# Three long VectorE products of a graph-attention kernel, each made in four operations

## The chip, the cores and the metric

The kernel runs on one core of a Trainium2 chip. A core has a matrix engine (TensorE, "PE" in the profile, with its weight loads as "PEld"), a vector engine (VectorE, "DVE"), an activation engine (ScalarE, "ACT"), a general engine (GpSimd, "POOL") and a synchronising engine that here only issues DMAs (SyncE, "SP"). The metric is the device time in microseconds of one whole launch: 3388.77 us for the kernel before, the median of three runs (3386.15 to 3389.04).

## What is computed

A graph of N = 3125 nodes with 128 features and E = 50000 edges, sorted by destination, goes through a block of two graph convolutions and then through five graph-attention layers with two heads. A layer of the second kind is, in the reference:

```python
edge_emb = edge_attr_full @ ew.T + eb                 # 16 attributes per edge
xw = x @ W
xj = xw[src].reshape(-1, H, D) + edge_emb.reshape(-1, H, D)
xi = xw[dst].reshape(-1, H, D)
alpha = einsum('ehd,hd->eh', xi, att_i) + einsum('ehd,hd->eh', xj, att_j)
alpha = leaky_relu(alpha, 0.2)
ea = exp(alpha - segment_max(alpha, dst)[dst])
alpha = ea / (segment_sum(ea, dst)[dst] + 1e-16)
aggr = segment_sum(xj * alpha[..., None], dst)
x_next = aggr.mean(axis=1) + b                        # relu between layers
```

So a layer needs, for each edge, the row of its source node (a gather), two attention numbers, an exponential relative to the largest of its destination, and a weighted sum over the edges of each destination.

## The kernel before

Edges stand in tiles of 128, one per partition; 391 tiles hold real edges. Four tiles make a group, and a chunk is 28 tiles, that is seven groups: `CH = [28] * 13 + [16, 11]`, so 15 chunks in a layer and 75 in the five layers. The destinations of one tile fall into a window of WIN = 24 nodes. `onehot` (128 x 392 x 24) says which node of its tile's window an edge goes to.

**GpSimd** fetches the rows. For each tile of a layer, in order, it issues an indirect DMA (line 510) that reads 128 rows of 130 numbers of `table` in HBM into one slot of `ring`, which has 60 slots. Before tile t with t >= 60 it waits at the first tile of each group until TensorE has summed the group that used the slot 60 tiles earlier (`sums`, line 508). Between the layers it adds two halves of S (line 517) and clears tiles of `acc` (line 495).

**ScalarE** copies, per tile, the window of destination terms out of `ai_rows` into `ai_win` (line 580; 28 copies per chunk), and makes the exponentials of a chunk (line 586).

**VectorE** makes the weights. All its work on a chunk is written out in one order:

- `windows_sum(layer, c, part)` in three parts. Part 0 multiplies the chunk's edge attributes `at` (k tiles x 16) by the two heads' vectors into `prod`, 2 x 28 x 16 = 896 numbers per partition (line 1087). Part 1 waits for ScalarE's windows and multiplies `ai_win` by `onehot`, 28 x 2 x 24 = 1344 numbers (line 1091). Part 2 reduces both, over the 16 attributes (line 1093) and over the 24 nodes (line 1094), tells ScalarE that `ai_win` is free (`win_used`), and adds the two (line 1096).
- `chain_scan` waits until all gathers of the chunk have landed (line 1101) and adds the rows' terms (line 1105 or 1108); then come maxima per destination by scans within and across partitions (`chain_scan`, `chain_rows`, `chain_cols`, lines 1111 to 1156).
- `chain_probs` waits for the exponentials, copies them into `est`, and makes the edge terms: attributes times weight, 28 x 2 x 16 = 896 numbers (line 1175). `weigh` then makes the weighted one-hots `pw` of a group (192 numbers, line 1161), which TensorE waits for.
- `add_group` waits for a group's sum in PSUM and adds it into `acc` (line 1200).

The work of chunk c+1 is laid between the groups of chunk c (lines 1228 to 1253): parts 0, 1 and 2 of `windows_sum` stand ahead of the adds of groups 0, 1 and 2, the scan after group 2, rows and columns after group 3, the probabilities after group 5. `weigh` runs four groups ahead of the adds, and six PSUM banks hold sums. For the two short chunks all three parts stand after group 0.

**TensorE** takes the groups in order (`aggregate`, lines 728 to 749): it waits for `weigh`'s semaphore, clears the bank (line 741), and does two products for each tile (lines 745 and 747); after some groups it makes a tile of the self terms (line 783). `link(ins)` on VectorE gives an instruction an increment of the semaphore `step` and makes the engine wait for it; `mark(ins)` gives the increment alone.

Of the kernel before, what the change touches and what calls it, by code (L numbers as in the profile page):

```python
# [5 lines left out]
ALU = mybir.AluOpType  # L6
# [4 lines left out]
AX = mybir.AxisListType.X  # L11

P = 128
# [3 lines left out]
H = 2  # L17
LAYERS = 5
FA = 16
# [6 lines left out]
WIN = 24  # L26
ROW = D + H
REG = 3
HF = H * FA
QD = 32  # L30
EC = HF + 2 * H
BIG = 1e30
# [14 lines left out]
TC = [sum(CH[:c]) for c in range(NC + 1)]  # L47
# [7 lines left out]
NAT = 3  # L55
# [42 lines left out]
def program(nc, x, src_rows, src_key, src_flat, dst_col, dst_next_col, dst_flat, dst_first,  # L98
            attr, W1, b1, W2, b2,
            weights, weightsT, attT, edge_w, edge_b, edge_woT, biases, edge_bias, out):  # L100
    with ExitStack() as ctx:
# [17 lines left out]
        onehot = sb("onehot", [P, TILES, WIN])  # L119
        S = sb("S", [P, NT, H * D])  # L120
        est = sb("est", [P, 2, K, EC])
        at = sb("at", [P, NAT, K, FA])
        ai_win = sb("ai_win", [P, K, H, WIN])
        prod = sb("prod", [P, H * K * FA])
# [7 lines left out]
        alpha = sb("alpha", [P, H, QB])  # L132
# [24 lines left out]
        v17 = sb("v17", [P, LAYERS, H, FA + 1])  # L157
# [15 lines left out]
        ee = bwd[:, :, :].rearrange("p h e -> p (h e)")[:, 0:H * K]  # L173
# [103 lines left out]
        step = sem("step")  # L277
# [58 lines left out]
        est_ready = sem("est_ready")  # L336
        acc_zero = sem("acc_zero")
        win_ready = sem("win_ready")
        win_used = sem("win_used")
# [469 lines left out]
        def _(v):  # L809
            steps = [0]  # L810

            def mark(ins):
                steps[0] += 1
                ins.then_inc(step, 1)
                return steps[0]

            def link(ins):
                v.wait_ge(step, mark(ins))
# [5 lines left out]
            V = nc.vector  # L824
# [7 lines left out]
            link(V.tensor_scalar(phi_mask[:, 0:1], iota_p, float(FA), None, ALU.is_lt))  # L832
            link(V.tensor_scalar(phi_mask[:, 1:2], iota_p, float(HF), None, ALU.is_lt))
            link(V.tensor_tensor(phi_mask[:, 1:2], phi_mask[:, 1:2], phi_mask[:, 0:1], ALU.subtract))
# [112 lines left out]
            for c in range(NPC):  # L947
                pick(c, n_e)
                b, ne = c % 2, n_e[:, c * PC:(c + 1) * PC]
# [71 lines left out]
            for g in range(GCN_G):  # L1021
# [3 lines left out]
                c, i = divmod(g, K // GRP)  # L1025
# [13 lines left out]
                win = acc[:, 0, bass.ds(base[0], GW)]  # L1039
# [40 lines left out]

            def windows_sum(layer, c, part):
                gc, k, hk = layer * NC + c, CH[c], H * CH[c]
                ts = slice(TC[c], TC[c + 1])
                win, pr = ai_win[:, 0:k, :, :], prod[:, 0:hk * FA].rearrange("p (h k f) -> p h k f", h=H, f=FA)
                if part == 0:
                    v.wait_ge(at_in[gc % NAT], 16 * (gc // NAT + 1))
                    link(V.tensor_tensor(pr, at[:, gc % NAT, 0:k, :].unsqueeze(1).broadcast_to((P, H, k, FA)),
                                         v17[:, layer, :, 0:FA].unsqueeze(2).broadcast_to((P, H, k, FA)), ALU.mult))
                if part == 1:
                    v.wait_ge(win_ready, gc + 1)  # L1090
                    link(V.tensor_tensor(win, win, onehot[:, ts, :].unsqueeze(2).broadcast_to((P, k, H, WIN)), ALU.mult))  # L1091
                if part == 2:
                    V.tensor_reduce(ee[:, 0:hk], prod[:, 0:hk * FA].rearrange("p (q f) -> p q f", f=FA), AX, ALU.add)
                    link(V.tensor_reduce(alpha[:, :, 0:k].rearrange("p h k -> p k h"), win, AX, ALU.add))  # L1094
                    v.sem_inc(win_used, 1)
                    link(V.tensor_tensor(alpha[:, :, 0:k], alpha[:, :, 0:k],
                                         ee[:, 0:hk].rearrange("p (h k) -> p h k", h=H), ALU.add))

# [67 lines left out]
            def chain_probs(layer, c):  # L1166
                gc, k, hk = layer * NC + c, CH[c], H * CH[c]
                es = est[:, c % 2, 0:k, :]
                v.wait_ge(exp_al, gc + 1)
                link(V.transpose(probs[:, :, :], dd[:, 0:H * QB].rearrange("p (h e) -> p h e", h=H)))  # L1170
                pr = probs[:, :, 0:k].rearrange("p h k -> p k h")
                done = mark(V.tensor_copy(es[:, :, HF:HF + H], pr))
                V.tensor_tensor(es[:, :, HF + H:EC], maxes[:, :, 0:k].rearrange("p h k -> p k h"),
                                last_col[:, TC[c]:TC[c + 1]].unsqueeze(2).broadcast_to((P, k, H)), ALU.mult)
                V.tensor_tensor(es[:, :, 0:HF].rearrange("p k (h f) -> p k h f", h=H),
                                at[:, gc % NAT, 0:k, :].unsqueeze(2).broadcast_to((P, k, H, FA)),
                                pr.unsqueeze(3).broadcast_to((P, k, H, FA)), ALU.mult).then_inc(est_ready, 1)
                v.wait_ge(step, done)
                for g in GC[c][0:2 if c else AHEAD]:
                    weigh(layer, g)  # L1180
# [22 lines left out]
            for layer in range(LAYERS):  # L1203
# [64 lines left out]
                for q in range(P // QD):  # L1268
                    ins = V.transpose(nsT[q * QD:(q + 1) * QD, :, :],
                                      acc[QD:2 * QD, 2, 0:NP].rearrange("p (j q n) -> p q j n", q=P // QD, n=QD)[:, q, :, :])  # L1270
# [22 lines left out]
                for j in range(NT):  # L1293
# [7 lines left out]
                    if not final and j >= 1:  # L1301
# [3 lines left out]
                    ins = V.scalar_tensor_tensor(out=yj, in0=yb[:, D:2 * D], scalar=c1[:, 1, j:j + 1],  # L1305
                                                 in1=yj, op0=ALU.mult, op1=ALU.add).then_inc(y_sb, 1)
# [71 lines left out]
```

## Time and profile before

| | |
|---|---|
| time, median of 3 runs | 3388.77 us (3386.15 to 3389.04) |
| span of the profiled execution | 3764.7 us, 48376 instructions |
| PE busy | 2439.0 us (65%) |
| POOL busy | 2210.5 us (59%) |
| DVE busy | 2004.0 us (53%) |
| ACT busy | 696.7 us (19%) |
| mean granted TensorE clock of the span | 0.537 |

The span is from the first to the last instruction of one execution recorded by the hardware profiler; the page gives no other time for that execution. It is 376 us longer than the median of the runs without the profiler, so the span and the metric are not the same thing. "Busy" leaves out waiting, semaphore and register instructions. A row of a group gives line, engine, operation, what it writes and reads, how often, then the time in which the group was busy and the mean of one, and the idle time ahead of it with what ended it. "Remote" is an end of waiting that the view can put down to no instruction of the core.

### The profile page before, as it was taken

To read this page: it belongs to the slowest core of one execution; us is meant where nothing else is said; L and a number is where in the kernel's file an instruction comes from. 1 tells how busy PE (TensorE), PEld (TensorE's weight loads), DVE (VectorE), ACT (ScalarE), POOL (GpSimd) and SP (SyncE) were. 2 spreads that over 40 slices of the span, in tenths; PEclk is the share of its full clock that TensorE was granted. 3 is DMA by queue.
4 is the path that set the end of the run, shared out by engine and by line. 5 is a ranking of instruction groups with operands and counts; after the bars stand their busy time and mean duration, and the time that the engine had idled before them with its cause. 6 is when DMAs were issued, how large, how long until landed. Compare 5 with 4: busy or idle time off the path is not lost.

```text
span 3764.7 us, 48376 instructions
## 1 busy us (share of the span) xinstructions
PE 2439.0 (65%) x13595; PEld 2001.4 (53%) x13595; DVE 2004.0 (53%) x6216; ACT 696.7 (19%) x3102; POOL 2210.5 (59%) x2357
## 2 busy tenths in 40 slices
PE   6779726666582766658276665837576582766668
PEld 6679615555461655547165554725455461655546
DVE  8955624554472555547255554725454472555456
ACT  0078511111121111112111111211111121111112
POOL 0067466666626766662666666266676626666661
PEclk8555555555565555556555555655555565555556
DMA  3212122222202222221222222022222202222221
GB/s 101 97 60 80 30 52 54 53 52 57 49 24 51 54 51 53 56 49 30 47 54 52 53 56 49 25 53 54 50 53 57 50 24 50 54 50 53 52 49 40
DMA packets 114121, 195.78 MB, mean 52 GB/s; under 512 B 39897, under 2 KB 77272, under 8 KB 113864
## 3 DMA queue, kind: packets, MB, share of 16 engines
q0 software_dynamic: 62560, 130.25, 15.2%
q1 hardware_dynamic: 51304, 62.42, 5.3%
q8 instruction: 122, 2.00, 0.2%
q14 instruction: 135, 1.11, 0.1%
HBM read 180.86 MB, written 11.67 MB: 51 GB/s over the span
## 4 chain that ended last, share of the span: by engine, by line
DVE 36%; PE 25%; another core or an unknown queue 20%; issue 13%; DVEq 3%; POOL 1%; ACT 1%; ACTq 1%; DMA 0%; POOLq 0%
PE bank L745 10%; PE bank L747 6%; DVE acc L1200 4%; DVE into L1143 2%; DVEq L1016 2%; PE bank L718 2%; DVE pw L1161 2%; DVE alpha L1094 2%; PE bank L741 2%; PE bank L783 2%; DVE fwd L1150 2%; DVE lanes L1129 2%; DVE prod L1072 1%; PE bank L766 1%
## 5 line engine op out<-in xcount | busy, mean ns | idle before, releaser
L510 POOL DMA_INDIRECT ring<-table,srci x1955 | 1941.2, 993 | 937.6 <-issue 556.4
L745 PE MATMUL bank<-pw,ring 128*128 128x48 f32 x3910 | 1210.9, 404 | 203.3 <-issue 201.8
L745 PEld LDWEIGHTS bank<-pw,ring 128*128 128x128 f32 x3910 | 1014.9, 314 | 302.9 <-issue 231.1
L1200 DVE TENSOR_TENSOR acc<-acc,bank 128x288 f32 x490 | 222.8, 455 | 1128.7 <-remote 857.3
L747 PE MATMUL bank<-onehot,est 128*36 128x24 f32 x3910 | 632.6, 243 | 222.9 <-issue 221.7
L741 PE MATMUL bank<-zeros 128*128 128x288 bf16 x490 | 208.5, 426 | 697.1 <-DVE pw L1161 438.7
L747 PEld LDWEIGHTS bank<-onehot,est 128*36 128x36 f32 x3910 | 391.2, 149 | 393.9 <-issue 226.6
L741 PEld LDWEIGHTS bank<-zeros 128*128 128x128 bf16 x490 | 55.4, 113 | 752.0 <-DVE pw L1161 453.3
L586 ACT ACTIVATE dd<-dd 128x66 f32<-128x66 f32 x75 | 19.4, 258 | 2163.4 <-DVE dd L1154 1177.9
L580 ACT COPY ai_win<-ai_rows 128x48 f32 x1955 | 336.3, 229 | 432.6 <-issue 410.5
L491 POOL TENSOR_TENSOR ring<-ring,acc 128x512 f32<-128x512 f32 x98 | 117.1, 1195 | 250.1 <-ACT ring L545 246.7
L517 POOL TENSOR_TENSOR S<-S 128x128 f32<-128x128 f32 x125 | 57.4, 459 | 323.6 <-ACT S L590 319.2
L783 PE MATMUL bank<-Wl,S 128*128 128x258 f32 x250 | 152.8, 697 | 50.1 <-issue 48.7
L718 PE MATMUL bank<-onehot,ring 128*128 128x24 f32 x784 | 172.2, 388 | 18.4 <-ACT ring L556 7.9
L718 PEld LDWEIGHTS bank<-onehot,ring 128*128 128x128 f32 x784 | 169.3, 331 | 21.1 <-DVE bank L1043 8.8
L1091 DVE TENSOR_TENSOR ai_win<-ai_win,onehot 128x1344 f32<-128x1344 f32 (+2 forms) x75 | 109.1, 1455 | 122.5 <-issue 101.2
L1161 DVE TENSOR_TENSOR pw<-onehot,est 128x192 f32<-128x192 f32 x490 | 160.0, 352 | 0.1
L556 ACT ACTIVATE ring<-ring,acc 128x128 f32<-128x128 f32 x392 | 124.3, 389 | 29.4 <-PE bank L718 24.7
L1143 DVE COPY into<-carry 2x96 f32<-2x96 f32 x300 | 93.6, 312 | 45.9 <-issue 33.8
L800 PE MATMUL bank<-El,acc 128*128 128x256 f32 x250 | 95.8, 470 | 23.8 <-DVE y L1305 20.0
L1094 DVE TENSOR_REDUCE alpha<-ai_win 128x56 f32<-128x1344 f32 (+2 forms) x75 | 108.6, 1448 | 0.0
L783 PEld LDWEIGHTS bank<-Wl,S 128*128 128x128 f32 x250 | 64.6, 308 | 70.3 <-issue 63.8
(214 smaller groups left out, 2610.1 us busy)
## 6 DMA issues: line engine op xcount, KB each, us to landing
ring<-table,srci POOLq DMA_INDIRECT x1955
ai_rows<-lo_dram SPq DMA_DIRECT2D x28, 896.0 KB, 4.3
at<-in_attr SPq DMA_DIRECT2D x65, 224.0 KB
table<-ring SPq DMA_DIRECT2D x15, 390.0 KB, 3.5
table<-ring SPq DMA_DIRECT2D x5, 325.0 KB, 3.4
result<-ring SPq DMA_DIRECT2D x24, 64.0 KB
x_mid<-ring SPq DMA_DIRECT2D x3, 384.0 KB, 2.7
table<-ring SPq DMA_DIRECT2D x5, 130.0 KB, 2.4
```

The source lines that it names most:

```text
L510: nc.gpsimd.indirect_dma_start(out=ring[:, slot(t), :], out_offset=None, in_=table, in_offset=bass.IndirectOffsetOnAxis(ap=srci[:, t:t + 1 ...
L556: ins = nc.scalar.activation(rows[:, g % 3, k, :], pre[:, g % 3, k, :], ACT.Relu, scale=n_e[:, t:t + 1])
L580: ins = nc.scalar.copy(ai_win[:, t - TC[c] + k, :, :], ai_rows[:, :, bass.ds(base[k], WIN)])
L718: ins = nc.tensor.matmul(total[:, at_k], rows[:, g % 3, k, :], onehot[:, t0 + k, :], start=False, stop=k == GRP - 1, skip_group_check=True)
L741: nc.tensor.matmul(total, zeros[:, 0:P], zeros[:, :], start=True, stop=False, skip_group_check=True)
L745: nc.tensor.matmul(wide[:, 0:H, at_k], ring[:, slot(t), 0:D], pw[:, g % DEEP, k, :, :], start=False, stop=False, skip_group_check=True)
L747: ins = nc.tensor.matmul(wide[0:EC, H, at_k], est[:, c % 2, t - TC[c], :], onehot[:, t, :], start=False, stop=k == n - 1, skip_group_check ...
L783: nc.tensor.matmul(bank[3][:, 0:H * D + H], S[:, j, D:2 * D], Wl[:, layer % 2, :], start=True, stop=True).then_inc(s_ps, 1)
L1094: link(V.tensor_reduce(alpha[:, :, 0:k].rearrange("p h k -> p k h"), win, AX, ALU.add))
L1143: ins = V.tensor_copy(into[i * QB:i * QB + H, :, :], carry[:, :, 1 + i:1 + P:NQB])
L1161: V.tensor_tensor(pw[:, g % DEEP, 0:n, :, :], onehot[:, t:t + n, :].unsqueeze(2).broadcast_to((P, n, H, WIN)), est[:, c % 2, k:k + n, HF:H ...
L1200: V.tensor_tensor(win, win, grp_sum(g).rearrange("p (r w) -> p r w", r=REG), ALU.add)\
```

## The change

Each of the three products is cut along the tiles of the chunk, at k/4, k/2 and 3k/4: for 28 tiles four operations of seven tiles. The reduction of the window product (line 1094) is cut in the same way and moved from part 2 into part 1, behind the product that it reads: product 0, product 1, sum 0, product 2, sum 1, product 3, sum 2, sum 3, where each sum waits for its product by the `step` semaphore. `win_used` goes with it. The attribute reduction (line 1093) and the last add stay in part 2; the reduction is now linked. What is computed is the same.

```diff
+WIN_PARTS = 4
                 if part == 0:
                     v.wait_ge(at_in[gc % NAT], 16 * (gc // NAT + 1))
-                    link(V.tensor_tensor(pr, at[:, gc % NAT, 0:k, :].unsqueeze(1).broadcast_to((P, H, k, FA)),
-                                         v17[:, layer, :, 0:FA].unsqueeze(2).broadcast_to((P, H, k, FA)), ALU.mult))
+                    cuts = [k * q // WIN_PARTS for q in range(WIN_PARTS + 1)]
+                    for a, b in zip(cuts, cuts[1:]):
+                        ins = V.tensor_tensor(pr[:, :, a:b, :],
+                                              at[:, gc % NAT, a:b, :].unsqueeze(1).broadcast_to((P, H, b - a, FA)),
+                                              v17[:, layer, :, 0:FA].unsqueeze(2).broadcast_to((P, H, b - a, FA)),
+                                              ALU.mult)
+                    link(ins)
                 if part == 1:
                     v.wait_ge(win_ready, gc + 1)
-                    link(V.tensor_tensor(win, win, onehot[:, ts, :].unsqueeze(2).broadcast_to((P, k, H, WIN)), ALU.mult))
+                    cuts = [k * q // WIN_PARTS for q in range(WIN_PARTS + 1)]
+
+                    def multiply(q):
+                        a, b = cuts[q], cuts[q + 1]
+                        return mark(V.tensor_tensor(win[:, a:b], win[:, a:b],
+                                                    onehot[:, TC[c] + a:TC[c] + b, :].unsqueeze(2)
+                                                    .broadcast_to((P, b - a, H, WIN)), ALU.mult))
+
+                    def add_up(q):
+                        a, b = cuts[q], cuts[q + 1]
+                        return V.tensor_reduce(alpha[:, :, a:b].rearrange("p h k -> p k h"), win[:, a:b], AX, ALU.add)
+
+                    done = multiply(0)
+                    for q in range(WIN_PARTS):
+                        following = multiply(q + 1) if q + 1 < WIN_PARTS else 0
+                        v.wait_ge(step, done)
+                        ins = add_up(q)
+                        done = following
+                    link(ins)
+                    v.sem_inc(win_used, 1)
                 if part == 2:
-                    V.tensor_reduce(ee[:, 0:hk], prod[:, 0:hk * FA].rearrange("p (q f) -> p q f", f=FA), AX, ALU.add)
-                    link(V.tensor_reduce(alpha[:, :, 0:k].rearrange("p h k -> p k h"), win, AX, ALU.add))
-                    v.sem_inc(win_used, 1)
+                    link(V.tensor_reduce(ee[:, 0:hk], prod[:, 0:hk * FA].rearrange("p (q f) -> p q f", f=FA), AX, ALU.add))
                     link(V.tensor_tensor(alpha[:, :, 0:k], alpha[:, :, 0:k],
                                          ee[:, 0:hk].rearrange("p (h k) -> p h k", h=H), ALU.add))
...
-                V.tensor_tensor(es[:, :, 0:HF].rearrange("p k (h f) -> p k h f", h=H),
-                                at[:, gc % NAT, 0:k, :].unsqueeze(2).broadcast_to((P, k, H, FA)),
-                                pr.unsqueeze(3).broadcast_to((P, k, H, FA)), ALU.mult).then_inc(est_ready, 1)
+                cuts = [k * q // WIN_PARTS for q in range(WIN_PARTS + 1)]
+                for a, b in zip(cuts, cuts[1:]):
+                    ins = V.tensor_tensor(es[:, a:b, 0:HF].rearrange("p k (h f) -> p k h f", h=H),
+                                          at[:, gc % NAT, a:b, :].unsqueeze(2).broadcast_to((P, b - a, H, FA)),
+                                          pr[:, a:b].unsqueeze(3).broadcast_to((P, b - a, H, FA)), ALU.mult)
+                ins.then_inc(est_ready, 1)
```

## Rows read from the trace of the kernel before

**Rows 1.** The table by stretches: busy us of each engine (instructions), clock, DMA share, GB/s.

```profile
core 0: us, PE busy (x) PEld busy (x) DVE busy (x) ACT busy (x) POOL busy (x), PEclk, DMA share, GB/s
0.00:475.40 475.40, 378.46 (x4045) 344.64 (x4046) 337.84 (x781) 199.68 (x651) 176.21 (x177) 0.57 0.22 74
475.40:1042.40 567.00, 332.22 (x1520) 264.83 (x1518) 265.23 (x821) 74.75 (x403) 389.36 (x391) 0.51 0.22 52
1042.40:1133.10 90.70, 78.61 (x388) 64.80 (x389) 68.02 (x282) 26.58 (x92) 20.43 (x50) 0.67 0.09 25
```

**Rows 2.** The table by stretches for the gathers (L510) alone, sum of five layers.

```profile
sum 2840.70, POOL 1941.15; mean POOL 388.23
```

**Rows 3.** The gathers by source line: shortest, median, longest in ns.

```profile
L510 POOL DMA_INDIRECT ring<-table,srci x1955: 942/947/2335, 475.5 to 3675.6; - x196
```

**Rows 4.** The page's group of the gathers.

```profile
L510 POOL DMA_INDIRECT ring<-table,srci x1955 | 1941.2, 993 | 937.6 <-issue 556.4 <-remote 288.6 <-PE bank L747 53.7
```

**Rows 5.** Who waited for whom: us in total, times, longest.

```profile
DVE acc L1200 <- remote: 857.3, 163, 9.8
POOL ring L510 <- issue: 556.4, 1825, 0.3
PE bank L741 <- DVE pw L1161: 438.7, 53, 68.8
```

**Rows 6.** VectorE in order of time, 1413.5 to 1422.5 us: start, duration, instructions.

```profile
1414.80 1.08 DVE L1175 TENSOR_TENSOR est<-at,probs 128x896 f32<-128x896 f32 x1
1415.80 0.62 DVE L1161 TENSOR_TENSOR pw<-onehot,est 128x192 f32<-128x192 f32 x2
...
1418.03 1.09 DVE L1087 TENSOR_TENSOR prod<-at,v 128x896 f32<-128x896 f32 x1
...
1420.56 1.55 DVE L1091 TENSOR_TENSOR ai_win<-ai_win,onehot 128x1344 f32<-128x1344 f32 x1
```

**Rows 7.** GpSimd in the same stretch.

```profile
1414.84 1.86 POOL L510 DMA_INDIRECT ring<-table,srci  x1 [0.30 <-issue]
...
1418.45 1.50 POOL L510 DMA_INDIRECT ring<-table,srci  x1 [0.30 <-issue]
1420.25 0.95 POOL L510 DMA_INDIRECT ring<-table,srci  x1 [0.30 <-issue]
1421.50 1.43 POOL L510 DMA_INDIRECT ring<-table,srci  x1 [0.30 <-issue]
```

**Rows 8.** VectorE's groups, shapes kept apart: busy us, mean ns of one.

```profile
L1161 DVE TENSOR_TENSOR pw<-onehot,est 128x192 f32<-128x192 f32 x485 | 158.5, 352 | 0.1
L1091 DVE TENSOR_TENSOR ai_win<-ai_win,onehot 128x1344 f32<-128x1344 f32 x65 | 100.8, 1551 | 122.3 <-issue 101.2 <-ACT ai_win L580 21.1
L1094 DVE TENSOR_REDUCE alpha<-ai_win 128x56 f32<-128x1344 f32 x65 | 100.4, 1545 | 0.0
L1087 DVE TENSOR_TENSOR prod<-at,v 128x896 f32<-128x896 f32 x65 | 71.0, 1093 | 5.2 <-remote 1.8 <-DVE acc L1191 1.4
L1175 DVE TENSOR_TENSOR est<-at,probs 128x896 f32<-128x896 f32 x65 | 70.5, 1084 | 0.0
```

**Rows 9.** VectorE in order of time, 1125 to 1222 us: the start of a layer.

```profile
1150.37 1.08 DVE L1087 TENSOR_TENSOR prod<-at,v 128x896 f32<-128x896 f32 x1
1179.25 1.56 DVE L1091 TENSOR_TENSOR ai_win<-ai_win,onehot 128x1344 f32<-128x1344 f32 x1 [27.79 <-issue]
...
1214.44 1.16 DVE L1161 TENSOR_TENSOR pw<-onehot,est 128x192 f32<-128x192 f32 x4
```

**Rows 10.** The table by stretches, one chunk of the second layer.

```profile
1380.30:1418.00 37.70, 23.10 (x108) 18.96 (x107) 20.90 (x67) 5.00 (x29) 25.68 (x26) 0.50 0.22 52
```

**Rows 11.** GpSimd: the 61st gather of the second layer.

```profile
1221.18 0.95 POOL L510 DMA_INDIRECT ring<-table,srci  x1 [12.04 <-PE bank L747]
```

**Rows 12.** Two products by source line: shortest, median, longest in ns.

```profile
L1087 DVE TENSOR_TENSOR prod<-at,v x75: 518/1091/1145, 485.0 to 3703.4; 128x896 f32<-128x896 f32 x65, 128x512 f32<-128x512 f32 x5, 128x352 f32<-128x352 f32 x5
L1091 DVE TENSOR_TENSOR ai_win<-ai_win,onehot x75: 707/1551/1559, 499.8 to 3703.9; 128x1344 f32<-128x1344 f32 x65, 128x768 f32<-128x768 f32 x5, 128x528 f32<-128x528 f32 x5
```

**Rows 13.** VectorE in order of time, behind the last gather of the first layer.

```profile
1042.58 0.69 DVE L1087 TENSOR_TENSOR prod<-at,v 128x512 f32<-128x512 f32 x1
1044.08 0.46 DVE L1200 TENSOR_TENSOR acc<-acc,bank 128x288 f32 x1 [0.81 <-PE bank L747]
...
1047.49 0.46 DVE L1200 TENSOR_TENSOR acc<-acc,bank 128x288 f32 x1 [1.82 <-PE bank L747]
```

More of the change, by code:

```diff
@@ L1082, in windows_sum @@
                 gc, k, hk = layer * NC + c, CH[c], H * CH[c]
-                ts = slice(TC[c], TC[c + 1])
                 win, pr = ai_win[:, 0:k, :, :], prod[:, 0:hk * FA].rearrange("p (h k f) -> p h k f", h=H, f=FA)
```

## The prediction

> **What bounds the kernel now.** I read the page first, then the table by stretches. The five attention layers are nearly the whole of it. Before them lie 475 us. Each layer is then a stretch of 391 gathers (567.0 us in the first layer) and a stretch without gathers of about 91 us [rows 1]. The five gather stretches add up to 2840.7 of the span's 3764.7 us [rows 2]; this is where a chunk's work is done and where the change acts.
>
> In that stretch GpSimd is the busiest engine, 389 of 567 us, against 332 for TensorE and 265 for VectorE [rows 1]. Its real share is larger. Ahead of 1825 of the 1955 gathers stands a gap of 0.30 us in which it waited for nothing (556.4 us / 1825), which its share of busy time leaves out [rows 5]. The median gather takes 0.947 us [rows 3], so GpSimd's own pace is 0.947 + 0.305 = 1.25 us a tile: 489 us for a layer's 391 tiles, 35.0 us for a chunk of 28. TensorE's work for a chunk is some 23 us and VectorE's some 21 us [rows 10].
>
> What are the other 78 us of 567? First, gathers that take longer than the median: (0.993 − 0.947) x 1955 = 90 us over the kernel, 18 us a layer [rows 3, 4]. Second, waits for a free ring slot: 288.6 + 53.7 us over the kernel, some 60 us a layer once the usual 0.30 us gap is taken off and the wait at the start (12.04 us in the second layer) is counted in [rows 4, 11].
>
> The second kind I put down mostly to the recording. The profiled span is 376 us over the median of the runs, and the rows show stalls of a kind no instruction explains: 857 us of VectorE's waiting ahead of its group adds ends "remote", 5.3 us each time [rows 5]. Suppose the plain run has no ring waits: its gather stretches take 5 x (489 + 18) = 2535 us and everything else 3389 − 2535 = 854 us, 8% below the 924 us (3764.7 − 2840.7) that it takes under the profiler. Suppose all ring waits are real: then everything else would have to shrink from 924 to 548 us, by 41%, though its engines are mostly busy there [rows 1]. The first is far more likely. So in the plain run GpSimd's issue of gathers sets the pace, and each microsecond taken off a gather is one off the kernel.
>
> **Why some gathers are long.** Set GpSimd and VectorE beside each other between 1414 and 1423 us [rows 6, 7]. The gather of 1414.84 took 1.86 us; the edge product had begun at 1414.80 and ended at 1415.88. The gather of 1418.45 took 1.50; the attribute product ended at 1419.12. The gather of 1421.50 took 1.43; the window product ended at 1422.11. In all three the gather ended 0.82 us after the product's end (1415.88 + 0.82 = 1416.70, 1419.12 + 0.82 = 1419.94, 1422.11 + 0.82 = 1422.93). So a gather that starts while such a product runs does its first 0.13 us, stops until the product has ended, and then does the other 0.82. Its delay is (product's end − gather's start) − 0.13. The gather of 1420.25, inside which the window product began (1420.56), took 0.95: a product that begins after the gather costs it nothing.
>
> Two more things stand in these rows. Right behind the edge product the two `weigh` products ran, from 1415.80 to 1416.42, and the waiting gather went on at 1415.88, not at 1416.42: when operations follow each other without a gap, the gather gets in between them. And a gather doesn't hold VectorE up: the window product of 1420.56 has its usual 1.55 us.
>
> The Trainium skill, "SBUF — State Buffer" ("SBUF: two separate sides"), describes a port pair that VectorE and GpSimd lock for a whole instruction, so that the loser blocks entirely. For the gather blocked by a product the trace agrees. For the other direction it doesn't: no 896-wide product took more than 1.145 us against a median of 1.091 [rows 12]. By that sentence, each added product could wait some 0.95 us behind a gather; nine more per chunk would be up to 8.6 us a chunk.
>
> **The gain.** A gather starts every 1.25 us. If its start falls evenly over the time, a product of duration d delays gathers by (d − 0.13)² / (2 x 1.25) on average; where d − 0.13 exceeds 1.25 one gather is always hit, by (d − 0.13) − 0.625. With the durations of rows 8: attributes 1.093 gives 0.37 us, edge terms 1.084 gives 0.36, window product 1.551 gives 0.80: 1.53 us a chunk. The seven `weigh` of 0.352 give 7 x 0.02 = 0.14, unchanged. The reductions read one array; I take them as harmless, since the formula with them in would exceed what the rows have.
>
> The parts: from 192 to 896 numbers a product gains 741 ns, 1.05 ns a number [rows 8]. So 224 numbers take 0.352 + 32 x 0.00105 = 0.386 us and 336 take 0.503. Four of 0.386 delay gathers by 4 x 0.256²/2.5 = 0.105 us, twice; four of 0.503 by 4 x 0.373²/2.5 = 0.22. Together 0.43 instead of 1.53 us a chunk.
>
> For the 65 full chunks that is 99 us now and 28 after; the ten short chunks add about 4 and 1. Saved: 74 us, if phases are even. The recorded execution gives the other estimate. It has 90 us in all; the three products' share by the formula is 1.53/1.67 = 92%, so 83 us, of which 72% goes: 60 us. Phases were not even there. I take the middle, 67 us. The ends: nothing, if the gather doesn't get in between, and about 83 us (all that the recorded execution has).
>
> **The cost on VectorE.** Twelve instructions more per full chunk (three for each of the products and three for the reduction). Four `weigh` in a row take 1.16 us [rows 9], so each after the first costs (1.16 − 0.352)/3 = 0.27: an operation starts 0.08 us before the last one ends. Four attribute parts take 3 x 0.306 + 0.386 = 1.30 us instead of 1.09; four window parts 3 x 0.42 + 0.50 = 1.77 instead of 1.55; the reductions the same again. In all 4 x 0.21 = 0.84 us a chunk, less about 0.1 for the link behind the window product, in place of which stand waits that the next part covers. Ends: 0.7, and 1.8 us if every added operation costs its fixed 0.15 us (1.093 − 896 x 0.00105). VectorE has 35 − 21 = 14 us free in a chunk [rows 10], so in the steady part this costs nothing. The reduction moves one group earlier: the add of group 1 comes 1.9 us later, but sums wait in six banks and `weigh` runs four groups ahead. If that cover is gone, see the second rival.
>
> The Trainium skill, "VectorE: DVE Perf Modes" (the TRN2 errata section), says the fixed cost is some 150 cycles (0.156 us) per instruction and advises tiles of at least 512 elements; all parts here are under that. By it the twelve would cost 1.9 us a chunk, 140 us over 75 chunks if they stood on the path. The rows of four in a row show half of it hidden.
>
> Where is VectorE on the path? At a layer's start chunk 0 is made alone. Its attribute product is done 28 us before the windows are ready [rows 9], so it hides; window product, reduction and edge terms add 0.6 us, which counts only if the 61st gather still waits [rows 11]: 0 to 3 us over five layers, I take 1. Behind the last gather of a layer come chunk 13's and 14's products, up to 2 x 0.84 us a layer where nothing covers; VectorE waits there 0.8 and 1.8 us for TensorE between its adds [rows 13], which covers about half or more: 0 to 8 us, I take 3.
>
> **Sum.** −67 + 1 + 3 = −63 us. The times of the terms come from the profiled execution of 3764.7 us. Against the median of the runs: 3388.8 − 63 = 3326 us. With the ends of the terms, the likeliest case has 3389 − 83 = 3306 to 3389 − 45 = 3344.
>
> **Rivals.**
>
> 1. *The ring waits are real.* TensorE and VectorE set the pace by their handover, GpSimd has slack, and a shorter gather only makes it wait longer for a slot. For it: 342 us of such waits [rows 4] and 439 us in which TensorE waits for `weigh` [rows 5]. Against it: the 41% above. If wholly true, nothing is gained: 3389 us, 3380 to 3395. If half true, about half: 3357.
>
> 2. *The handover pays for the parts (slower).* Same place, but here the price is counted: TensorE starts a chunk when `weigh` has come, behind the edge terms. Its idle 439 us ahead of line 741 ends with `weigh`. If that handover, and not GpSimd, ends last in every chunk, then between 0.21 us (edge terms alone) and 0.74 us (all of VectorE's addition) is paid in 75 chunks: 16 to 55 us, taken at 0.6, 3389 + 45 = 3434. It decides once a chunk takes TensorE and VectorE more than GpSimd's 35.0 + 1.7 = 36.7 us. In the recorded chunks it did (37.7 in the one shown [rows 10]), with the profiler's stalls.
>
> 3. *The port isn't given up between the parts.* Then a chain of four parts blocks like one operation of 1.30 us: (1.30 − 0.13)²/2.5 = 0.55 instead of 0.37, twice, while the window products alternate with reductions and fall to some 0.3 from 0.80. Sum 1.4 instead of 1.53: 75 x −0.1 + 4 = −4 us, 3385. Against it is the gather that resumed at 1415.88 [rows 6, 7].
>
> 4. *A gather holds up the products* for its whole length, the sentence of the skill's page above. With some six of nine added parts hit by 0.95 us, VectorE's chunk goes from 21 to 27 us, still under 35, but chunk 0 and the end pay some 6 us each: 5 x 12 = 60 us, which eats the gain: 3326 + 60 = 3386.
>
> **Chances.** Forecast 0.77 (with the partly true first rival in it); rival 1 in full 0.09; rival 2 0.08; rival 3 0.04; rival 4 0.02. A difference under 0.2%, 7 us, can't be told from none here. Faster: 0.77 and a little of rivals 3 and 4, 0.80. Same: 0.11. Slower: 0.09. The range reaches from 3306 up to 3372, where three quarters of the gain is absorbed; outside lie rivals 1 to 4 in full and a little below, under 0.2 together.
>
> **What would show it.** In the profile after: products of 0.386 and 0.503 us; no gather delayed by more than 0.4 us in the steady part; the mean gather down from 993 to about 962 ns. The gaps of 0.30 us unchanged. The recorded span may fall by less than the plain time, since ring waits there can take up part of it. I am wrong if the mean gather falls but the time doesn't (rival 1 or 2), if delays of 1 us and more remain (rival 3), or if the parts themselves are drawn out (rival 4).

## The result, and the profile after

The changed kernel takes 3314.4 us (median of 4 runs, 3312.2 to 3315.7) against 3387.9 us before: ratio 0.9784, 95% interval 0.9771 to 0.9798, that is 73 us faster (68 to 78). The forecast was 3326 us.

The recorded execution of 3764.7 us, from which the rows ahead of the prediction come, had stalls that no later one has, so the comparison here is with a second recorded execution of the unchanged kernel (experiment 1), whose span is 3386.7 us.

The page of the changed kernel, its span and the chain of waits by engine:

```profile
span 3313.8 us, 49276 instructions
POOL 51%; issue 19%; DVE 16%; PE 10%; DMA 2%; ACT 1%; DVEq 1%; POOLq 0%; ACTq 0%
```

Half of the chain is GpSimd, and a fifth is "issue", nearly all of it the 0.30 us gaps ahead of its gathers. The gathers after, as the page's group and by source line (shortest, median, longest):

```profile
L511 POOL DMA_INDIRECT ring<-table,srci x1955 | 1876.5, 960 | 633.5 <-issue 583.0 <-DMA table<-ring 39.2 <-PE bank L748 11.3
L511 POOL DMA_INDIRECT ring<-table,srci x1955: 940/944/1682, 475.5 to 3242.6; - x196
```

The mean gather is 0.960 us, where [rows 4] have 0.993 and the undisturbed kernel before 1.004. The longest is 1.68 instead of 2.3 us [rows 3], and no wait for a ring slot is left beyond the usual gap. VectorE's groups after, against [rows 8]:

```profile
L1100 DVE TENSOR_TENSOR ai_win<-ai_win,onehot 128x336 f32<-128x336 f32 x260 | 124.5, 499 | 22.5 <-ACT ai_win L581 22.5
L1106 DVE TENSOR_REDUCE alpha<-ai_win 128x14 f32<-128x336 f32 x260 | 123.3, 495 | 0.0
L1089 DVE TENSOR_TENSOR prod<-at,v 128x224 f32<-128x224 f32 x260 | 84.3, 386 | 2.3 <-DVE acc L1216 0.3
L1199 DVE TENSOR_TENSOR est<-at,probs 128x224 f32<-128x224 f32 x260 | 83.9, 383 | 0.0
```

The parts last what was worked out (0.386 and 0.503 us) or a few ns less, so they aren't drawn out by gathers. The same two engines side by side, VectorE first, then GpSimd, as in [rows 6] and [rows 7]:

```profile
1409.04 1.29 DVE L1199 TENSOR_TENSOR est<-at,probs 128x224 f32<-128x224 f32 x4
1410.24 0.62 DVE L1183 TENSOR_TENSOR pw<-onehot,est 128x192 f32<-128x192 f32 x2
...
1417.09 0.50 DVE L1100 TENSOR_TENSOR ai_win<-ai_win,onehot 128x336 f32<-128x336 f32 x1
```

```profile
1409.25 0.98 POOL L511 DMA_INDIRECT ring<-table,srci  x1 [0.30 <-issue]
1410.54 1.15 POOL L511 DMA_INDIRECT ring<-table,srci  x1 [0.30 <-issue]
...
1417.12 1.28 POOL L511 DMA_INDIRECT ring<-table,srci  x1 [0.30 <-issue]
```

The gather of 1409.25 begins in the first part of the edge terms' train of 1.29 us and loses 0.03 us (its 0.98 less the median of 0.944), where a whole product begun at 1409.04 would have cost it 0.74. That of 1410.54 meets the second `weigh` and loses 0.2. The gather of 1417.12 begins 0.03 us into a window part and loses 1417.59 − 1417.12 − 0.13 = 0.34 us, and 1.28 − 0.944 is that. Of the 1955 gathers only two lose more than 0.4 us; they come up under experiment 11.

### The profile page after: what moved, and what is told of

It reads as the page before. It is cut to its first block, busy times and chain, and to the rows that moved or that the text cites. A ratio compares the mean times of both kernels' runs of the same rounds, so it can differ in the third digit from the quotient of the medians.

```text
span 3313.8 us, 49276 instructions
## 1 busy us (share of the span) xinstructions
PE 2404.6 (73%) x13595; PEld 1979.7 (60%) x13595; DVE 2061.6 (62%) x7116; ACT 669.5 (20%) x3102; POOL 2145.4 (65%) x2357
## 3 DMA queue, kind: packets, MB, share of 16 engines
q14 instruction: 142, 1.16, 0.1%
## 4 chain that ended last, share of the span: by engine, by line
POOL 51%; issue 19%; DVE 16%; PE 10%; DMA 2%; ACT 1%; DVEq 1%; POOLq 0%; ACTq 0%
POOL ring L511 47%; PE bank L746 5%; POOL ring L492 3%; PE bank L748 2%; DMA ring<-table,srci 2%; DVE prod L1073 2%; DVE ring L848 2%; DVE y L1324 1%; DVE y L1330 1%; POOL ring L487 1%; PE bank L742 1%; PE bank L719 1%; DVE ai_rows L941 1%; DVE acc L1225 1%; PE bank L784 1%
## 5 line engine op out<-in xcount | busy, mean ns | idle before, releaser
L511 POOL DMA_INDIRECT ring<-table,srci x1955 | 1876.5, 960 | 633.5 <-issue 583.0
L748 PE MATMUL bank<-onehot,est 128*36 128x24 f32 x3910 | 619.1, 246 | 0.0
L748 PEld LDWEIGHTS bank<-onehot,est 128*36 128x36 f32 x3910 | 382.5, 150 | 177.6
L1127 DVE TENSOR_TENSOR alpha<-alpha,ring 128x56 f32<-128x56 f32 (+7 forms) x75 | 18.0, 240 | 684.4 <-DMA ring<-table,srci 684.3
L581 ACT COPY ai_win<-ai_rows 128x48 f32 x1955 | 309.1, 228 | 58.0 <-issue 22.7
L1100 DVE TENSOR_TENSOR ai_win<-ai_win,onehot 128x336 f32<-128x336 f32 (+1 forms) x300 | 136.5, 475 | 22.6 <-ACT ai_win L581 22.5
L1106 DVE TENSOR_REDUCE alpha<-ai_win 128x14 f32<-128x336 f32 (+1 forms) x300 | 135.0, 471 | 0.0
```

What stands on the lines that cost most here:

```text
L511: nc.gpsimd.indirect_dma_start(out=ring[:, slot(t), :], out_offset=None, in_=table, in_offset=bass.IndirectOffsetOnAxis(ap=srci[:, t:t + 1 ...
L581: ins = nc.scalar.copy(ai_win[:, t - TC[c] + k, :, :], ai_rows[:, :, bass.ds(base[k], WIN)])
L748: ins = nc.tensor.matmul(wide[0:EC, H, at_k], est[:, c % 2, t - TC[c], :], onehot[:, t, :], start=False, stop=k == n - 1, skip_group_check ...
L1100: return mark(V.tensor_tensor(win[:, a:b], win[:, a:b], onehot[:, TC[c] + a:TC[c] + b, :].unsqueeze(2) .broadcast_to((P, b - a, H, WIN)), ...
L1106: return V.tensor_reduce(alpha[:, :, a:b].rearrange("p h k -> p k h"), win[:, a:b], AX, ALU.add)
```

## The experiments

Each experiment gives the median of its own runs, then the ratio to the kernel before on the same chip with its 95% interval. How many microseconds faster or slower is worked out from the ratio, times 3389. A gather's delay is what it takes beyond the median gather of its own trace.

**1. The kernel before once more.**

> The kernel before, unchanged, for a second recorded execution. The first one spanned 3764.7 us while the runs took 3388. Blocking theory (a product delays a gather that starts inside it, and GpSimd sets the pace): span within 3 us of 3386, a layer's gather stage about 489 + 21 = 510 us instead of 567, no waits for a ring slot, mean gather 0.947 + 0.055 = 1.00 us (107 us of delays in all by even phases). Rival (the ring waits are real): the stage keeps its 60 us of ring waits and the time comes out short elsewhere.

Measured: 3388.6 us, span 3386.7. Its page and its list of who waited for whom:

```profile
span 3386.7 us, 48376 instructions
L510 POOL DMA_INDIRECT ring<-table,srci x1955 | 1962.8, 1004 | 632.5 <-issue 569.3 <-DMA table<-ring 38.2 <-PE bank L747 25.0
```

```profile
DVE alpha L1105 <- DMA ring<-table,srci: 757.2, 65, 17.1
PE bank L741 <- DVE pw L1161: 638.4, 70, 37.9
```

The 289 us of ring waits and the 857 us "remote" of [rows 4, 5] are gone. VectorE now waits 65 times, 11.6 us each, for the landing of a chunk's last gather, and TensorE waits for VectorE. So GpSimd sets the pace. The five gather stages, before and after (stretch from the first to the last gather; the sum's second number is GpSimd's busy time):

```profile
475.30:985.70 510.40, 391.40 (x391) 0.51 0.25 58
...
sum 2557.70, POOL 1962.75; mean POOL 392.55
```

```profile
475.40:970.10 494.70, 375.70 (x391) 0.51 0.26 60
...
sum 2471.30, POOL 1876.52; mean POOL 375.30
```

The stages are 86.4 us shorter, and GpSimd's busy time in them is 86.2 us shorter: the same microseconds. The spans differ by 72.9, so 13.5 us were given back between the stages. The delays before come to (1.004 − 0.946) x 1955 = 113 us, 0.946 being this execution's median gather; after, (0.960 − 0.944) x 1955 = 31.

**2 to 4. One product cut at a time.** The edits are the change's own, each alone; the window product goes with its reduction.

> Only the attribute product is made in four operations. Blocking theory: delays fall by (0.37 - 0.105) x 65 + 0.5 = 18 us, VectorE's 0.2 us a product cost at most 1 us at the layers' ends: 3370 to 3372 us. Rival (the gain of the whole change comes from the earlier reduction and the earlier release of the windows, an order of VectorE's work): 0, 3388. Rival (a part costs VectorE time on the path): 3388 + up to 15.

> Only the window product is made in four operations, with its reduction cut and moved ahead as in the whole change. Blocking theory: delays fall by (0.80 - 0.22) x 65 + 1 = 39 us, cost 1 to 2 us: about 3350 us. Rival (the order of VectorE's work is the gain): all of it, 3314. Rival (handover to TensorE pays for the parts): 3388 or above.

> Only the edge terms are made in four operations. They stand right ahead of the weights that TensorE waits for. Blocking theory: delays fall by (0.36 - 0.105) x 65 + 0.5 = 17 us, cost at most 1: about 3372 us. Rival (order of work): 0, 3388. Rival (handover to TensorE): 75 x 0.21 = 16 us slower, 3404.

Measured: attributes alone 3385.0 us, 0.9985 (0.9976 to 0.9994), 5 us faster where 18 were expected; windows alone 3368.3, 0.9937 (0.9924 to 0.9951), 21 where 39 were expected; edge terms alone 3334.6, 0.9837 (0.9823 to 0.9850), 55 us faster where 17 were expected. Both rivals fall with the last number: the handover to TensorE pays nothing, and the order of the reduction isn't the gain. The split by product was badly wrong. For this table each delayed gather of a trace is put down to the VectorE operation that lay longest beside it (us over all 1955 gathers; a window part and its reduction count as one, and `all` has the other operations too):

| kernel | attributes | windows | edge terms | `weigh` | all |
|---|---|---|---|---|---|
| before | 32 | 39 | 29 | 10 | 114 |
| attributes cut | 8 | 57 | 28 | 10 | 107 |
| windows cut | 31 | 15 | 31 | 10 | 92 |
| edge terms cut | 11 | 34 | 1 | 2 | 53 |
| changed kernel | 3 | 19 | 1 | 2 | 31 |

Cutting the attributes took 24 us off their own delays and put 18 on the window product's. Cutting the edge terms took 28 off their own, and 29 off those of the attributes and `weigh`, which had not been touched. One chunk of the kernel before shows why, VectorE and then GpSimd:

```profile
1399.36 1.08 DVE L1175 TENSOR_TENSOR est<-at,probs 128x896 f32<-128x896 f32 x1
...
1401.26 0.62 DVE L1161 TENSOR_TENSOR pw<-onehot,est 128x192 f32<-128x192 f32 x2
1402.59 1.09 DVE L1087 TENSOR_TENSOR prod<-at,v 128x896 f32<-128x896 f32 x1
...
1405.11 1.55 DVE L1091 TENSOR_TENSOR ai_win<-ai_win,onehot 128x1344 f32<-128x1344 f32 x1
```

```profile
1399.92 1.34 POOL L510 DMA_INDIRECT ring<-table,srci  x1 [0.30 <-issue]
1401.56 1.13 POOL L510 DMA_INDIRECT ring<-table,srci  x1 [0.30 <-issue]
1403.00 1.49 POOL L510 DMA_INDIRECT ring<-table,srci  x1 [0.30 <-issue]
...
1406.05 1.43 POOL L510 DMA_INDIRECT ring<-table,srci  x1 [0.30 <-issue]
```

And a chunk of the kernel with only the edge terms cut:

```profile
1418.18 1.29 DVE L1178 TENSOR_TENSOR est<-at,probs 128x224 f32<-128x224 f32 x4
...
1421.61 1.09 DVE L1088 TENSOR_TENSOR prod<-at,v 128x896 f32<-128x896 f32 x1
...
1424.14 1.54 DVE L1092 TENSOR_TENSOR ai_win<-ai_win,onehot 128x1344 f32<-128x1344 f32 x1
```

```profile
1418.71 0.97 POOL L511 DMA_INDIRECT ring<-table,srci  x1 [0.30 <-issue]
1419.98 0.96 POOL L511 DMA_INDIRECT ring<-table,srci  x1 [0.30 <-issue]
...
1422.50 1.02 POOL L511 DMA_INDIRECT ring<-table,srci  x1 [0.31 <-issue]
...
1425.07 1.43 POOL L511 DMA_INDIRECT ring<-table,srci  x1 [0.30 <-issue]
```

VectorE waits for a landing in 65 of the 75 chunks, so its order has a fixed place against the gathers: the edge terms begin 0.7 us into one (47 of 65 chunks). A gather held up by them starts the next ones later, and one of those then begins early in the attribute product: delays 0.39, 0.18, 0.54 and 0.48 us, 1.6 in all. With the edge terms cut the gathers stay on time, and one meets the attribute product 0.2 us before its end: 0.03, 0.01, 0.07 and 0.48. A blocked gather ends 0.82 us behind the product, wherever it began, so a delay moves every later meeting. Even phases gave the sum over the products here (113 us worked out, 113 found) and no product's share of the gain. Experiments 5 and 6 show that the sum isn't fixed by the lengths of the products either.

**5 and 6. Nothing cut, useless work added.** That explanation makes an odd forecast, so it was tried. The edit of experiment 5 (512 numbers; experiment 6 has 128):

```diff
+                V.tensor_reduce(ee[:, 0:32], prod[:, 0:512].rearrange("p (q f) -> p q f", f=FA), AX, ALU.add)
                 V.tensor_tensor(es[:, :, HF + H:EC], maxes[:, :, 0:k].rearrange("p h k -> p k h"),
```

> The kernel before, all products whole, plus one useless reduction of 512 numbers (about 0.6 us of VectorE, one array read, its result is overwritten unread) ahead of the edge terms in every chunk. Fixed-phase theory: VectorE's order starts at the landing of a chunk's last gather, so each product meets the gathers at a fixed offset; the edge terms began 0.70 us into a gather (47 of 65 chunks) and delayed the next by 0.70 + 1.08 - 1.25 - 0.13 = 0.40 us, and the later ones followed from that. Moved by 0.6 us they begin with a gather and end before the next: delays of a chunk worked through with the rule fall from 1.66 to 1.14 us, 65 x -0.51 = -33 us, and up to 5 us come back behind each layer's last gather: about 3361 us, faster than before although work is only added. Rival (even phases; splitting is what helps): no gain, 3389 to 3394. Rival (VectorE's work before the weights is on the path): 75 x 0.6 = 45 us slower, 3434.

> The same with a useless reduction of 128 numbers, about 0.2 us. Fixed-phase theory: the edge terms still run into the next gather, now by 0.6 instead of 0.4 us; delays worked through with the rule rise from 1.66 to 1.86 us a chunk: 65 x 0.2 = 13 us, plus 1 to 2 behind the layers: about 3404 us, slower than with the three times longer useless operation. Even phases: 3389 to 3391. VectorE on the path: 75 x 0.2 = 15 us, 3404 as well, so this run counts only together with the 0.6 us one.

Measured: with 0.6 us more work per chunk 3363.1 us, 0.9916 (0.9902 to 0.9929), 28 us faster; with 0.2 us more 3401.1 us, 1.0029 (1.0020 to 1.0038), 10 us slower. Both came out the way that was expected, the first within 1 us of its forecast gain and the second 5 us less slow than forecast. The delays, 76 and 125 us in the traces, are near what the rule gave (1.14 and 1.86 us for each of 65 chunks: 74 and 121). The three products are as long as before in both, so the same products can cost 76 us or 125. The chunk that explains it, in the faster one:

```profile
1425.47 0.68 DVE L1173 TENSOR_REDUCE bwd<-prod 128x32 f32<-128x512 f32 x1
1426.19 1.09 DVE L1176 TENSOR_TENSOR est<-at,probs 128x896 f32<-128x896 f32 x1
```

```profile
1428.44 1.12 POOL L510 DMA_INDIRECT ring<-table,srci  x1 [0.30 <-issue]
1429.87 1.50 POOL L510 DMA_INDIRECT ring<-table,srci  x1 [0.30 <-issue]
...
1432.93 1.42 POOL L510 DMA_INDIRECT ring<-table,srci  x1 [0.30 <-issue]
```

Gathers begin every 1.25 us, so ahead of 1428.44 at 1427.19 and 1425.94. Pushed back by the useless reduction, the edge terms (1426.19 to 1427.28) begin behind the one and end less than 0.13 us into the other: both keep their 0.95 us and aren't among the long ones shown.

**7. Only the reductions cut**, four operations each in their old place (shortened):

```diff
-                    V.tensor_reduce(ee[:, 0:hk], prod...)
-                    link(V.tensor_reduce(alpha..., win, AX, ALU.add))
+                    for a, b in zip(cuts, cuts[1:]):
+                        V.tensor_reduce(ee...[:, :, a:b], pr[:, :, a:b, :], AX, ALU.add)
+                    for a, b in zip(cuts, cuts[1:]):
+                        ins = V.tensor_reduce(alpha[:, :, a:b]..., win[:, a:b], AX, ALU.add)
+                    link(ins)
```

> Products whole; both reductions of part 2 are made in four operations each, in their old place: six instructions and 0.42 us of VectorE more a chunk, nothing else. They come before the wait for the gathers' landing, so they move no phase. Blocking theory (only operations that read two arrays delay gathers, and VectorE has slack): 3389, within 2 us but for up to 1 us a layer behind the last gather (3394). Rival (reductions block too, and cutting them helps): 10 to 40 us faster. Rival (added instructions cost): 75 x 0.42 = 31 us slower, 3420.

Measured: 3392.8 us, 1.0004 (0.9995 to 1.0013); delays 115 us, where the kernel before has 114. Six more instructions a chunk cost nothing that can be measured, and cutting reductions gains nothing.

**8. The change with the window reduction whole and in part 2.**

> The whole change except that the window product's reduction stays in one piece in part 2 (four window parts back to back). Blocking theory: delays nearly those of the whole change, since the products are cut in the same way: 3314 within 8 us; chunk 0 and the layers' ends save a little. Rival (moving and interleaving the reduction, and freeing the windows earlier, brings a part of the gain): 3330 or above.

Measured: 3314.2 us, 0.9775 (0.9761 to 0.9788). The reordering of the reduction and the earlier release of the windows bring nothing.

**9 and 10. A useless product, or a useless reduction, where VectorE is idle.** Put ahead of the wait for the gathers (the product is shown, shortened; the reduction of experiment 10 reads the same 896 numbers of `prod` and writes 56):

```diff
+                if 0 < c < NC - 2:
+                    V.tensor_tensor(prod[:, 0:896], prod[:, 0:896], onehot...[:, 0:896], ALU.mult)
                 v.wait_ge(gath[c % NGATH], 16 * in_class(c, layer))
```

> The kernel before, plus one useless product of 896 numbers (two arrays read, 1.09 us) in each of chunks 1 to 12 of a layer, 60 in all, put where VectorE has nothing to do: right ahead of its wait for a chunk's gathers, which lasts about 10 us. Blocking theory: it begins 0.6 us into a gather (43 of 60) and delays the next by about 0.6 + 1.09 - 1.25 - 0.13 = 0.3 us; over the 60 places 24 us: 3389 + 24 = 3413. Rival (VectorE's work in its idle time is free): 3389.

> The same with a useless reduction of 896 numbers (one array read, 1.08 us) in the same 60 places. Blocking theory, for operations that read two arrays only: nothing, 3389 within 3 us. Rival (any long operation of VectorE holds a gather up): 3413, like the product.

Measured: product 3410.6 us, 1.0068 (1.0055 to 1.0082), 23 us slower, with 24 us of delays beside the added products; reduction 3384.2 us, 0.9991 (0.9982 to 1.0000), no slower. VectorE has the time for either; what costs is that the product holds up a gather:

```profile
1416.56 1.09 DVE L1102 TENSOR_TENSOR prod<-prod,onehot 128x896 f32<-128x896 f32 x1
1417.22 1.24 POOL L510 DMA_INDIRECT ring<-table,srci  x1 [0.30 <-issue]
```

The gather loses 1417.65 − 1417.22 − 0.13 = 0.30 us. This is the cleanest pair for the mechanism: same place, same length, and only the operation that reads two arrays costs. The two also differ in what they write, 896 numbers against 56. The trace of experiment 1 speaks against writing as the cause: the group adds write 288 numbers, with one array read from `acc` in SBUF and the other from PSUM. Of 70 gathers that began inside such an add and at least 0.19 us before its end, none lost more than 0.04 us, nor did any of the 129 that began so inside one of the two reductions. One of each kind, the operation and then the gather:

```profile
573.65 0.46 DVE L1200 TENSOR_TENSOR acc<-acc,bank 128x288 f32 x1 [0.56 <-DVE alpha L1096]
573.72 0.94 POOL L510 DMA_INDIRECT ring<-table,srci  x1 [0.30 <-issue]
...
1410.26 1.54 DVE L1094 TENSOR_REDUCE alpha<-ai_win 128x56 f32<-128x1344 f32 x1
1410.27 0.95 POOL L510 DMA_INDIRECT ring<-table,srci  x1 [0.30 <-issue]
```

The Trainium skill ("SBUF — State Buffer", "SBUF: two separate sides") names a VectorE operation with two SBUF inputs against a GpSimd operation that reads SBUF as a case in which one blocks the other. The runs agree, if the issue of an indirect DMA counts as such an operation. The same section tells of a probe in which a `tensor_tensor` did not stall a DMA issued by GpSimd; here the product does hold up the issue, by 0.30 us in the rows above.

**11. Seven parts instead of four** (`WIN_PARTS = 7`).

> The changed kernel with seven operations of four tiles for each product. Even phases: delays of 0.27 instead of 0.43 us a chunk, 10 us less; VectorE's 0.6 us more a chunk costs some 4 us behind the layers: about 3308. Fixed phases, worked through with the rule on the measured offsets: 0.44 instead of 0.32 us a chunk, 8 us more, and the same 4: about 3326. Either way under 0.4% of the four-part kernel.

Measured: 3318.7 us, 0.9797 (0.9784 to 0.9811), no better than four parts (0.9784), and halfway between the two forecasts. Delays are 32 us, where four parts have 31, and the stretches behind the five stages take 2.6 us more in all. The traces show where the shorter parts lose. VectorE and then GpSimd, with seven parts and with four:

```profile
522.68 1.16 DVE L1183 TENSOR_TENSOR pw<-onehot,est 128x192 f32<-128x192 f32 x4
522.48 2.18 POOL L511 DMA_INDIRECT ring<-table,srci  x1 [0.30 <-issue]
```

```profile
1656.87 1.15 DVE L1183 TENSOR_TENSOR pw<-onehot,est 128x192 f32<-128x192 f32 x4
1657.16 1.68 POOL L511 DMA_INDIRECT ring<-table,srci  x1 [0.30 <-issue]
```

The first gather ends at 524.66, which is 0.82 us behind the fourth `weigh` (522.68 + 1.16 = 523.84); it had begun with an edge part and didn't get in behind that part or behind any `weigh` before the last. The second began in the second of four `weigh` and waited for the fourth (1658.02 + 0.82 = 1658.84), 0.54 us more than if it had got in behind the second. So a gather does not always get in between. Counted over the traces: with seven parts, 16 gathers were passed over by one to four operations of 128 or 192 numbers, which cost 9.2 of the 32 us. In the changed kernel it is two gathers, each passed over in a train of four `weigh`, 1.1 of the 31 us. All 49 gathers there that met a part of 224 or 336 numbers with another product right behind it got in behind that part. The 9.2 us are about the 10 us that even phases had forecast as the gain of seven parts; that they are why it stayed out is likely, and no run separates them. What decides whether a gather is passed over, no run shows: in experiment 4 three gathers that began 0.03 us into a `weigh` of such a train got in behind it, and one didn't. The Trainium skill's advice of at least 512 elements per operation ("VectorE: DVE Perf Modes", the errata section) would have spoken against four parts already; here parts of 224 and 336 gain, since GpSimd and not VectorE sets the pace, and going on to 128 and 192 gains nothing.

**12. Whole again at the end of a layer** (the two lines that set the number of parts):

```diff
+                parts = WIN_PARTS if c < NC - 1 else 1      # windows_sum
+                parts = WIN_PARTS if c < NC - 2 else 1      # chain_probs
```

> The changed kernel, but the products of a layer's last chunk, and the edge terms of the one before it, are whole again: no gather is left there to be held up, and VectorE's work is on the path. Theory (a part of the 13 us given back behind the last gathers is VectorE's time for parts): 0.6 to 0.9 us a layer, 3 to 4 us: 3310 to 3311. Rival (given back because VectorE and TensorE start no earlier when the last gathers come sooner): 3314.

Measured: 3306.6 us, 0.9771 (0.9756 to 0.9785): the fastest kernel of all by its median, though its interval overlaps the changed kernel's. By the ratios it is 4 us faster than the changed kernel, as expected; by the medians 8, and by the two traces 9: its gather stages are as long (2470.7 us in all) and the rest of its span is shorter (833.3 instead of 842.5). One layer gained over 4 us there, two about 2 and two under 1, for which the trace gives no single cause. So the products' part in what is given back is likely, and its size isn't settled.

## Why the prediction was right, point by point

**What bounds the kernel: right, though from a bad witness.** The profile shown had GpSimd waiting for TensorE. The argument that this was no property of the kernel rested on one subtraction (what would be left for everything else), and experiment 1 bears it out: no ring waits. The cause given was wrong, though: it isn't recording that stalls the kernel, since the span of 3313.8 us belongs to an execution that took 3315.7; the stalls were that one execution's.

**Why gathers are long: right.** The rule (product's end − gather's start − 0.13) was read off three gathers. In the trace of experiment 1, all 249 gathers that one of the four products delayed by over 0.1 us end 0.81 to 0.83 us behind that product. With the rule, experiments 5, 6 and 9 were forecast at −28, +15 and +24 us and came out at −28, +10 and +23. The whole gain hung on the claim that a gather gets in between operations that follow without a gap. It held for all 49 gathers that met the parts, the 0.98 us gather above among them. It isn't general, as the trains of `weigh` and the seven parts of experiment 11 show; it had been read off one gather.

**The gain: the term "middle of 74 and 60, 67 us" was too small.** Delays fell by 82 us, from 113 to 31. Even phases, with `weigh` and the short chunks, gave 113 and 39, within 8 us each. That is partly luck: the phases are not even, as experiments 2 to 4 show, and experiments 5 and 6 moved the sum to 76 and 125 us with the three products whole. The 60 came from the disturbed execution, in which GpSimd's waits kept the products and the gathers in other phases (90 us of delays). It should have had no weight once its ring waits were held to be foreign. Some 4 us more came from a median gather of 0.944 instead of 0.946 us, which no run explains.

**The cost behind the last gather: the term "I take 3" was too small,** 13.5 us with the other terms between the stages. The end of the first layer, before and after, by VectorE:

```profile
992.40 0.52 DVE L1087 TENSOR_TENSOR prod<-at,v 128x352 f32<-128x352 f32 x1
...
995.18 0.20 DVE L1105 TENSOR_TENSOR alpha<-alpha,ring 128x22 f32<-128x22 f32 x1
...
1015.22 0.45 DVE L1200 TENSOR_TENSOR acc<-acc,bank 128x288 f32 x1 [2.12 <-PE bank L747]
```

```profile
978.30 0.72 DVE L1089 TENSOR_TENSOR prod<-at,v 128x64 f32<-128x64 f32 x4
...
981.67 0.20 DVE L1127 TENSOR_TENSOR alpha<-alpha,ring 128x22 f32<-128x22 f32 x1
...
1001.91 0.46 DVE L1225 TENSOR_TENSOR acc<-acc,bank 128x288 f32 x1 [2.12 <-PE bank L748]
```

The last gather ended at 985.63 and at 970.02. The last chunk's products begin 6.8 us behind it before and 8.3 after; from there to the scan it takes 2.8 and 3.4; the last add begins 29.6 and 31.9 us behind it. So 0.6 us is VectorE's own work for the parts, as worked out. Another 1.0 us is not work: the scan of chunk 12, which starts the chain of the last chunks, comes 32.4 instead of 33.4 us ahead of the last gather's end. The 27 gathers behind it have lost most of their delays (0.3 us in all instead of 1.2), and that gain is worth nothing at the end. The prediction left this out. The other 0.7 of the 2.3 us lies elsewhere between that scan and the last add. In experiment 12 the last add of this layer comes 30.9 us behind the last gather: with the last chunk's products whole, 1.0 of the 2.3 us is gone and 1.3 stay. The cost at the layers' starts (1 us) did not show: no wait for a ring slot is left there.

**The two misses partly cancel**: −82 − 4 + 13 = −73 where −67 + 4 = −63 was forecast. The time is 12 us under the forecast and inside the range.

**The rivals.** 1 and 2 (TensorE's handover) fall with experiments 1, 4 and 7; 3 (no gap between parts) with the 49 gathers that got in behind a part, though shorter operations do pass gathers over; 4 (gathers hold up products) with the parts' durations.

## What to carry to other kernels

Where GpSimd issues indirect DMAs back to back and sets the pace, look for long VectorE operations that read two arrays beside them: cut them. Turning them into operations that read one should do as well; experiment 10 speaks for it, and no run here tried it on the products themselves. Don't cut too short: trains of operations of 128 or 192 numbers made gathers wait for several of them. An edit that only moves VectorE by a fraction of a gather gained 28 us and lost 10 us here, so judge a cut by the sum of all delays, and never take one product's gain from a run in which others were still whole. What is saved just ahead of a stage's end is worth only what the chain behind it can start earlier.

## What the runs showed of the hardware that was not expected

- 0.6 us of useless VectorE work in each chunk made the kernel 28 us faster, and 0.2 us made it 10 us slower.
- VectorE's 60 useless products in its idle time cost 23 us; 60 reductions of the same size cost nothing that can be measured.
- A gather that a product delayed by over 0.1 us ended 0.81 to 0.83 us behind the product's end, wherever it had begun (249 gathers of experiment 1). Its end and the starts of all later gathers follow from the product's end, and not from its own start.
- In a train of short products a waiting gather can be passed over: four `weigh` ran ahead of the gather of 522.48 in experiment 11, which took 2.18 us.
- A VectorE add with one array in PSUM delayed none of the 70 gathers that began inside it, and a reduction none of 129.
